# Squares averaged in two fp32r products and clamps of two operations, in a block of time mixing and a gated layer

## The reference

```python
xn = layernorm(x)
# time mixing (rwkv): shifted = rows one step later, zero in the first
k = (xn * mk + shifted * (1 - mk)) @ Wk       # v and r alike, with mv and mr
r = sigmoid(r_in @ Wr)
# per channel, over 512 steps, with td = -exp(decay), tf:
#   running maximum mx, numerator num and denominator den
#   out = (exp(mx - m) * num + exp(k + tf - m) * v) / (exp(mx - m) * den + exp(k + tf - m))
s = (r * out) @ Wo
# gated layer, expert 0 alone
h = relu(xn @ w1 + b1); y = xn + h @ w2 + b2
n = (y - mean(y)) * rsqrt(var(y) + eps) * gamma + beta
result = x + s * silu(n)
```

## Time and profile before

| what | us |
|---|---|
| median of 3 runs (lowest to highest) | 123.34 (123.24 to 123.43) |
| profiled execution, its own time | 122.89 |
| its span, first to last instruction | 121.0 |
| TensorE busy | 105.6 |
| VectorE busy | 96.4 |
| ScalarE busy | 95.0 |
| GpSimd busy | 79.8 |

### The profile page before, as it was taken

The page is one execution under the profiler, slowest core; times in us unless marked ns, Lnnn a source line. Parts: engine busy times, 40 slices in busy tenths (PEclk is TensorE's granted clock), DMA queues, the critical chain, the costliest instruction groups (busy, mean ns, idle before and its releaser), DMA issues. The chain is left out here.

```text
span 121.0 us, 1604 instructions
## 1 busy us (share of the span) xinstructions
PE 105.6 (87%) x336; PEld 56.7 (47%) x336; DVE 96.4 (80%) x199; ACT 95.0 (79%) x155; POOL 79.8 (66%) x104
## 2 busy tenths in 40 slices
...
GB/s 112 270 312 250 12 3 0 5 0 0 0 3 3 0 0 0 0 0 0 0 0 0 87 93 1 0 0 0 0 3 0 3 0 86 1 87 87 5 105 155
DMA packets 9449, 5.09 MB, mean 42 GB/s; under 512 B 480, under 2 KB 9184, under 8 KB 9440
## 3 DMA queue, kind: packets, MB, share of 16 engines
...
q10 hardware_dynamic: 560, 0.40, 1.3%
...
## 5 line engine op out<-in xcount | busy, mean ns | idle before, releaser
L632 PE MATMUL bank<-hid,w_c 128*128 128x512 f32 x64 | 31.4, 594 | 0.0
L581 PE MATMUL bank<-mixed,w_in 128*128 128x512 f32 x48 | 25.4, 624 | 1.7 <-DVE prod L792 0.6
L468 ACT ACTIVATE hid<-bank,vec 128x512 f32<-128x512 f32 x32 | 21.4, 681 | 2.3 <-PE bank L603 1.9
L601 PE MATMUL bank<-xT_hi,w_hi 128*128 128x512 f32 x28 | 16.5, 588 | 5.3 <-POOL xT_lo L356 5.3
L712 DVE SCALAR_TENSOR_TENSOR mixed<-step_x,vec,bank 128x511 f32<-128x511 f32 x24 | 17.5, 736 | 1.1 <-POOL step_x L365 1.1
L632 PEld LDWEIGHTS bank<-hid,w_c 128*128 128x128 f32 x64 | 12.2, 194 | 10.9 <-issue 9.7
L736 DVE TENSOR_TENSOR_SCAN den<-e_keep,bank 128x512 f32<-128x512 f32 x8 | 9.7, 1216 | 8.2 <-ACT e_keep L512 3.9
L389 POOL TENSOR_SCALAR gap_max<-gap,td 128x512 f32<-128x512 f32 x8 | 12.5, 1561 | 3.8 <-DVE gap L729 3.8
L581 PEld LDWEIGHTS bank<-mixed,w_in 128*128 128x128 f32 x48 | 8.4, 194 | 11.9 <-issue 8.8
L382 POOL TENSOR_SCALAR gap_min<-gap,td 128x512 f32<-128x512 f32 x8 | 12.5, 1561 | 1.9 <-DVE gap L729 1.9
L365 POOL TENSOR_TENSOR step_x<-xT 128x512 f32<-128x512 f32 x8 | 9.0, 1127 | 6.4 <-ACT xT L460 6.3
...
...
## 6 DMA issues: line engine op xcount, KB each, us to landing
...
```

Of the source, the lines that this page charges most:

```text
L468: act.activation(hid[b % 2][:, f, :], ps(f"up{f}", b)[:, :], ACT.Relu, bias=vec[:, B1_COLUMN + f:B1_COLUMN + f + 1]).then_inc(done[f"hid{f ...
L581: pe.matmul(ps(name, b)[:, :], w_in[:, which, :], mixed[b % 2][:, which, :], start=True, stop=True).then_inc(done[name], 1)
L601: pe.matmul(dst, hi, xT_hi[n][:, :], start=True, stop=False)
L632: ins = pe.matmul(ps("z", b)[:, :], w2_c[:, f, :], hid[b % 2][:, f, :], start=False, stop=last, skip_group_check=True)
```

## The change

Four things change together. First, for batches 0 to 6 the squares are split by GpSimd as the activations are: `sq_hi` is the square rounded to fp32r, `sq_lo` the rest, also stored as fp32r, and `var` becomes two fp32r products with `averager_r`, an fp32r copy of the averager, which add up in one bank. The halves of batch 7 keep the single fp32 product. Second, the two clamps are written with two operations each: a minimum and then a maximum, where the one that isn't needed compares with the largest fp32 number. Third, each `z` chunk has a semaphore of its own; `hid` of a chunk waits for that chunk's product of two batches ago, and `sq` for the last chunk in TensorE's list. Fourth, the lists of all four engines and the bank table are new.

The lists, in full but for that of ScalarE, whose start is shown:

```diff
     "pe": """
-        T:0 up3:0 b2m up2:0 k:0 T:1 up0:0 up1:0 v:0 k:1 up1:1 up0:1 up2:1 z0:0 z1:0 T:2 up3:1 z2:0 z0:1
-        z1:1 z3:0 up3:2 r:0 z3:1 z2:1 k:2 var:0 up2:2 up0:2 v:1 up1:2 z2:2 T:3 z0:2 var:1 s:0 z1:2 r:1
-        v:2 z3:2 up3:3 up2:3 up0:3 r:2 T:4 k:3 up1:3 z0:3 z2:3 var:2 z1:3 k:4 z3:3 up3:4 up0:4 var:3
-        up1:4 s:1 T:5 back:0 up2:4 v:3 back:1 z1:4 v:4 z0:4 up3:5 up1:5 z3:4 z2:4 T:6 s:2 r:3 r:4 k:5
-        up2:5 var:4 up1:6 up2:6 up0:5 v:5 T:7 k:6 z0:5 s:3 z2:5 up0:6 z1:5 z3:5 r:5 up3:6 z2:6 k:7 var:5
-        z1:6 up3:7 z0:6 up1:7 z3:6 up0:7 back:2 var:6 v:6 s:4 up2:7 back:3 v:7 z0:7 back:4 z1:7 z2:7 r:6
-        r:7 z3:7 s:5 var.a:7 var.b:7 back:5 s:6 s.a:7 back:6 s.b:7 back.a:7 back.b:7
+        T:0 up3:0 b2m up1:0 k:0 up0:0 T:1 v:0 up2:0 k:1 up2:1 up0:1 up1:1 up3:1 z3:0 T:2 r:0 z2:0 z1:0
+        z0:0 z3:1 z2:1 up0:2 z0:1 z1:1 up2:2 v:1 k:2 var:0 up1:2 z0:2 up3:2 T:3 z1:2 var:1 z2:2 v:2 r:1
+        z3:2 up0:3 up3:3 up1:3 up2:3 T:4 k:3 z3:3 r:2 z1:3 k:4 s:0 var:2 z2:3 z0:3 up3:4 up0:4 s:1 up2:4
+        T:5 v:3 z3:4 var:3 back:0 z2:4 back:1 z0:4 up1:4 v:4 up2:5 up0:5 z1:4 r:3 T:6 up3:5 r:4 up1:5
+        k:5 v:5 s:2 var:4 z1:5 up3:6 up2:6 z0:5 back:2 T:7 z2:5 s:3 up0:6 z3:5 up1:6 k:6 up0:7 r:5 z3:6
+        k:7 var:5 up2:7 z2:6 z0:6 z1:6 up3:7 up1:7 s:4 v:6 var:6 back:3 z3:7 s:5 back:4 v:7 z2:7 z1:7
+        z0:7 r:6 r:7 var.a:7 var.b:7 back:5 s:6 back:6 s.a:7 s.b:7 back.a:7 back.b:7
     """,
     "act": """
-        ln_exp ve:0 rs:0 xT:0 neg_td w1_hi ve:1 rs:1 hid3:0 xT:1 hid0:0 hid2:0 wo hid1:0 v_sb:0 ve:2
-        rs:2 e_keep:0 hid1:1 hid0:1 e_new:0 hid2:1 e_new:1 e_keep:1 xT:2 ln_den:0 hid3:1 ln_den:1
-        silu_set th_g:0 th_a:0 hid3:2 th_a:1 sq:0 th_g:1 th_r:0 ln_exp ln_var:0 hid2:2 rstd2:0 hid0:2
...
+        ln_exp ve:0 rs:0 wo neg_td xT:0 w1_hi ve:1 rs:1 xT:1 hid3:0 ve:2 rs:2 v_sb:0 hid1:0 hid2:0
+        hid0:0 e_new:0 hid2:1 hid0:1 e_keep:0 hid3:1 e_new:1 e_keep:1 xT:2 hid1:1 ln_den:0 ln_den:1
+        silu_set th_g:0 th_a:0 sq:0 th_a:1 hid0:2 th_r:0 th_g:1 sq:1 hid2:2 v_sb:1 ln_exp ln_var:0
...
     "dve": """
-        bnA:0 bnB:0 aggr1:0 norm1:0 bn:1 aggr1:1 ink:0 w2_sum cols bn:2 bn:3 aggr1:2 mx:0 inv:0 aggr1:3
-        ink:1 gap:0 inr:0 mx:1 bn:4 gap:1 inv:1 den:0 inr:1 den:1 aggr1:4 rel:0 ink:2 rel:1 inv:2 bn:5
-        dev:0 adev:0 wkv:0 aggr1:5 gated:0 mx:2 inr:2 gap:2 bn:6 zn:0 bn:7 aggr1:6 aggr1:7 dev:1 den:2
-        adev:1 wkv:1 rel:2 zn:1 inv:3 prod:0 ink:3 gated:1 inr:3 dev:2 adev:2 mx:3 wkv:2 gap:3 ink:4
-        gated:2 inv:4 mx:4 den:3 zn:2 gap:4 inr:4 rel:3 prod:1 res:0 den:4 zn:3 ink:5 res:1 rel:4 inv:5
-        dev:3 adev:3 wkv:3 dev:4 adev:4 wkv:4 gated:3 prod:2 gated:4 mx:5 gap:5 inr:5 ink:6 inv:6 zn:4
-        den:5 mx:6 rel:5 inr:6 prod:3 ink:7 dev:5 adev:5 gap:6 wkv:5 gated:5 mx:7 gap:7 den:6 inr:7 zn:5
-        inv:7 res:2 den:7 prod:4 rel:6 zn:6 res:3 rel:7 dev:6 adev:6 res:4 wkv:6 dev:7 gated:6 prod:5
-        adev:7 wkv:7 res:5 gated:7 prod:6 zn.a:7 zn.b:7 res:6 prod.a:7 prod.b:7 res.a:7 res.b:7
+        bnA:0 bnB:0 aggr1:0 norm1:0 bn:1 aggr1:1 ink:0 bn:2 w2_sum bn:3 aggr1:2 cols aggr1:3 inv:0 mx:0
+        ink:1 gap:0 bn:4 mx:1 inr:0 gap:1 inv:1 den:0 bn:5 den:1 inr:1 rel:0 rel:1 bn:6 aggr1:4 bn:7
+        dev:0 adev:0 ink:2 wkv:0 aggr1:5 gated:0 inv:2 inr:2 mx:2 gap:2 zn:0 aggr1:6 aggr1:7 dev:1 den:2
+        adev:1 zn:1 wkv:1 rel:2 inv:3 gated:1 ink:3 inr:3 dev:2 mx:3 ink:4 adev:2 gap:3 wkv:2 mx:4 gap:4
+        prod:0 gated:2 inr:4 zn:2 den:3 inv:4 prod:1 den:4 rel:3 inv:5 res:0 zn:3 ink:5 res:1 rel:4
+        dev:3 adev:3 wkv:3 dev:4 adev:4 gated:3 wkv:4 inr:5 mx:5 gap:5 gated:4 inr:6 prod:2 inv:6 den:5
+        zn:4 res:2 rel:5 prod:3 ink:6 ink:7 dev:5 mx:6 adev:5 gap:6 wkv:5 mx:7 gap:7 gated:5 inv:7 zn:5
+        den:6 inr:7 den:7 rel:6 prod:4 res:3 zn:6 res:4 rel:7 dev:6 prod:5 adev:6 wkv:6 dev:7 adev:7
+        gated:6 wkv:7 res:5 gated:7 prod:6 zn.a:7 zn.b:7 res:6 prod.a:7 prod.b:7 res.a:7 res.b:7
     """,
     "pool": """
-        d:0 w1_lo nm:1 fix:0 norm1:1 w2_c d:1 xT_hi:1 fix:1 xT_lo:1 gmax:0 nm:2 gmin:0 norm1:2 gmin:1
-        gmax:1 dv:0 d:2 xT_hi:2 xT_lo:2 keep:0 fix:2 norm1:3 keep:1 gmax:2 gmin:2 dv:1 d:3 xT_hi:3 nm:4
-        fix:3 xT_lo:3 norm1:4 dv:2 keep:2 xT_hi:4 d:4 fix:4 gmin:3 gmax:3 xT_lo:4 norm1:5 norm1:6 gmax:4
-        gmin:4 norm1:7 xT_hi:5 d:5 xT_lo:5 dv:3 keep:3 dv:4 keep:4 xT_hi:6 fix:5 xT_lo:6 d:6 fix:6
-        gmin:5 gmax:5 xT_hi:7 dv:5 d:7 keep:5 fix:7 gmax:6 xT_lo:7 gmin:6 gmin:7 gmax:7 dv:6 keep:6 dv:7
-        keep:7
+        d:0 w1_lo nm:1 fix:0 norm1:1 w2_c nm:2 d:1 xT_hi:1 fix:1 xT_lo:1 gmin:0 gmax:0 norm1:2 gmin:1
+        gmax:1 dv:0 d:2 fix:2 xT_hi:2 xT_lo:2 keep:0 sq_hi:0 norm1:3 sq_lo:0 sq_hi:1 sq_lo:1 keep:1 dv:1
+        gmax:2 gmin:2 nm:4 xT_hi:3 d:3 xT_lo:3 norm1:4 fix:3 dv:2 keep:2 d:4 sq_hi:2 fix:4 sq_lo:2
+        xT_hi:4 gmin:3 xT_lo:4 gmax:3 gmax:4 norm1:5 gmin:4 sq_hi:3 sq_lo:3 xT_hi:5 d:5 xT_lo:5 dv:3
+        norm1:6 keep:3 dv:4 keep:4 fix:5 sq_hi:4 sq_lo:4 xT_hi:6 d:6 xT_lo:6 gmin:5 gmax:5 norm1:7 dv:5
+        fix:6 xT_hi:7 d:7 xT_lo:7 keep:5 sq_hi:5 fix:7 sq_lo:5 gmax:6 gmin:6 gmin:7 gmax:7 sq_hi:6
+        sq_lo:6 dv:6 keep:6 dv:7 keep:7
     """,
...
```

The bank table is rewritten; in it `b2m` is followed by `v:0` in its bank, where `z:1` followed before, and a check of the bank is added ahead of `b2m`. The rest of the diff:

```diff
@@ -138,6 +141,7 @@
 
         ident = sb("ident", P, P)
         averager = sb("averager", P, P)
+        averager_r = sb("averager_r", P, P, dt=FP32R)
         vec = sb("vec", P, NV)
         neg_td = sb("neg_td", P, 1)
         td = sb("td", P, 1)
@@ -187,6 +191,8 @@
         gated = pair("gated", P, T)
         hid = pair("hid", P, NF, T)
         sq = pair("sq", P, T)
+        sq_hi = pair("sq_hi", P, T, dt=FP32R)
+        sq_lo = pair("sq_lo", P, T, dt=FP32R)
         ln_var = pair("ln_var", P, T)
         rstd2 = pair("rstd2", P, T)
         zn = pair("zn", P, T)
@@ -211,7 +217,7 @@
                   "mx", "gap", "gmin", "gmax", "e_new", "e_keep", "den", "ln_den", "rel",
                   "th_g", "th_a", "keep", "dv", "dev", "adev", "wkv", "th_r", "gated", "s"]
                  + [f"up{f}" for f in range(NF)] + [f"hid{f}" for f in range(NF)]
-                 + ["z", "sq", "var", "ln_var", "rstd2", "zn", "silu", "prod", "back", "res"])
+                 + [f"z{f}" for f in range(NF)] + ["sq", "sq_hi", "sq_lo", "var", "ln_var", "rstd2", "zn", "silu", "prod", "back", "res"])
         done = {n: sem(f"done_{n}") for n in STEPS}
         stored = [sem(f"stored_{n}") for n in range(2)]
         EDGES = 11
@@ -242,6 +248,10 @@
             elif previous:
                 for step in FREED_BY[previous[0]]:
                     after(eng, step, previous[2], previous[1])
+
+        def chunks_of(b):
+
+            return [name for name, _, i in tokens("pe") if name in CHUNKS and i == b]
 
         def cut(half):
             return {"": slice(0, T), "a": slice(0, T // 2), "b": slice(T // 2, T)}[half]
@@ -309,6 +319,8 @@
                                base=0, pattern=[[-1, P]], channel_multiplier=1).then_inc(prep["ident"], 1)
             pool.memset(eps[:, :], LN_EPS).then_inc(prep["consts"], 1)
             pool.memset(averager[:, :], 1.0 / H).then_inc(prep["consts"], 1)
+            pool.wait_ge(prep["consts"], 2)
+            pool.tensor_copy(averager_r[:, :], averager[:, :]).then_inc(prep["consts"], 1)
 
             def center_w2():
                 pool.wait_ge(prep["w2_sum"], 1)
@@ -379,14 +391,16 @@
                 once(pool, b, "cols", 4)
                 after(pool, "gap", b)
                 after(pool, "e_new", b - 2)
-                pool.tensor_scalar(gap_min[n][:, :], gap[n][:, :], td[:, :], None, ALU.min).then_inc(done["gmin"], 1)
+                pool.tensor_scalar(gap_min[n][:, :], gap[n][:, :], td[:, :], -FP32_MAX,
+                                   ALU.min, ALU.max).then_inc(done["gmin"], 1)
 
             def upper(b):
                 n = b % 2
                 once(pool, b, "cols", 4)
                 after(pool, "gap", b)
                 after(pool, "e_keep", b - 2)
-                pool.tensor_scalar(gap_max[n][:, :], gap[n][:, :], td[:, :], None, ALU.max).then_inc(done["gmax"], 1)
+                pool.tensor_scalar(gap_max[n][:, :], gap[n][:, :], FP32_MAX, td[:, :],
+                                   ALU.min, ALU.max).then_inc(done["gmax"], 1)
 
             def value_steps(b):
                 n = b % 2
@@ -403,7 +417,20 @@
                 after(pool, "dev", b - 2)
                 pool.tensor_scalar(keep[n][:, 1:], th_g[n][:, :], -0.5, 0.5, ALU.mult, ALU.add).then_inc(done["keep"], 1)
 
-            steps = {"w1_lo": w1_low, "w2_c": center_w2, "nm": minus_mean_rows, "norm1": normalise, "xT_hi": high_part,
+            def square_high(b):
+                n = b % 2
+                after(pool, "sq", b)
+                after(pool, "var", b - 2)
+                pool.tensor_copy(sq_hi[n][:, :], sq[n][:, :]).then_inc(done["sq_hi"], 1)
+
+            def square_low(b):
+                n = b % 2
+                after(pool, "sq_hi", b)
+                after(pool, "var", b - 2)
```

(38 more changed lines are left out.)

32 lines of the change are left out of this document (18 added, 14 removed).

## The result

The changed kernel takes 112.56 us (112.39 to 112.66, four runs) against 123.37 of before: a ratio of 0.912, 95% interval 0.911 to 0.914, so 10.8 us less. I had forecast 117.3 and a range of 114.5 to 121.8. The direction was right, and the gain is nearly twice what I took. The profiled execution took 112.47, with a span of 110.6. Where some executions of a kernel ran in a slower state of the chip, the times and ratios here leave them out.

What follows compares the result with a forecast made beforehand. It took GpSimd's queue in two places, TensorE's slower clock behind them, and TensorE with ScalarE from 60 on to bound the kernel. Of 11.2 us, ScalarE's cap left 6.0: 123.3 - 6.0 = 117.3, range 114.5 to 121.8.

Steps and rivals of the forecast that it cites:

- The price of the clamp: On GpSimd, a two-operation clamp takes 0.66 us instead of 1.56, judged by the nearest rows in form; 16 save 14.4.
- The first and second wait: TensorE's waits for `xT_lo` of batches 2 and 4, behind GpSimd's clamps: 2.57 goes and 1.89 all but goes.
- The slow clock: TensorE's lower granted clock after its two long waits: 1.68 and 1.70 us lost, to go with the waits.
- The averages: Squares' average on TensorE, batches 0 to 6: two fp32r products replace one fp32, 0.39 less each, 2.7 us in all.
- The sum: Of 11.2 us to be had on TensorE, 6.0 kept, since ScalarE's and VectorE's work doesn't shrink and ScalarE caps the gain.
- my own formula: Middle, 20 to 105 us: ScalarE's 73.5 busy divided by its busy share; at 93% it lasts 79.0, a gain of 6.0.
- My inventory of 11.2: TensorE's possible savings: 2.7 averages, 2.57, 1.89 and 0.67 waits for `xT_lo`, 1.68 and 1.70 slow clock.
- The signs: Expected profile: clamps 0.6 to 0.8, average records 0.24 apart, `xT_lo` waits under 1.5, clock above 0.98, ScalarE above 90%.
- the cap of 93%: ScalarE, 86% busy from 20 to 105 us, was allowed 93% over the whole middle, limiting the gain to 6.0.
- The slow clamp with the split squares: Rival on GpSimd: clamps keep 1.56 while squares add 13.1 to 13.7 us; near 128, chance 0.13.
- Squares that come late: Rival: clamps fast, but squares delayed in GpSimd's queue cost 4 plus 1.7 slow clock; 121.5 to 123, chance 0.12.
- Collisions: Rival: `sq_lo` and the cast on GpSimd meet VectorE's scan, 4.7 us more GpSimd work; 119, chance 0.15, gain kept.

Runs made afterwards that it cites:

- The forms: Changed kernel with another clamp form in each of batches 2 to 6, for durations alone; one execution, 125.58 us, a time that means nothing.
- filling the waits: Kernel before with 9 and 7 useless small products in TensorE's two long waits for `xT_lo`; 122.22 us, ratio 0.993.

## Why the prediction was wrong

*The price of the clamp* was right (0.69 for 0.66), its reason wrong. I wrote that the form of two operations was the nearest row. The forms show that the pair decides; by my reason a maximum then a minimum would be as fast, and it takes 2.0. The Trainium skill's best loop ("GPSIMD Engine Reference", §3.1), 0.77 for 512 elements, was above both 0.62 and 0.69 as measured.

*The first and second wait* went as worked out, the first to about half a microsecond in place.

*The slow clock* at 1.68 + 1.70 was a mis-sized term: 0.9 as measured by filling the waits.

*The averages* shortened as predicted on TensorE (0.46 for the two records in place of 0.86), but the 2.7 were not to be had: with unsplit squares the new lists take 112.2, no more than with split ones.

*The sum* has the step that failed: "ScalarE is thus the engine that caps the gain, and I take 6.0". I took ScalarE's busy share of 86% as its own property and allowed it 93%. Much of its idle time was made by the clamps, 8.5 us of it in the list of waits, of which I had used for ScalarE only the 1.5 for `var`; the change took 7.2 of the 8.5 away. Its share rose to 96.6%. At that share my own formula gives 73.5 / 0.966 = 76.1, a gain of 8.9 in the middle. The other 1.5 us of the span came outside it, where the sum had nothing: 0.8 is less busy time of ScalarE, the rest less idle time. My inventory of 11.2 was near the measured 10.8 by luck: 8.5 for waits and clock was at most 7.2, 2.7 for the averages was about nothing, and 4.2 from the other clamps, most likely through ScalarE, was missing.

*The signs* that I named for the changed kernel came out as written but for the 0.24 between the two records: clamps at 0.69, no wait for `xT_lo`, a clock of 1.000, ScalarE above 90%. They test the clamps and the two waits, and none of them tests the cap of 93%.

*The rivals.* The slow clamp with the split squares: 128 forecast; with the new lists it is 123.2, no slower than before, and in the old lists 133.2. Squares that come late: true of the old lists (122.5), where the price was 10.7 and not 4; the new lists avoid it. Collisions exist: in the changed kernel a `sq_hi` at 27.30 took 1.27 where 0.61 is usual, beside VectorE's scan of two tiles, and another at 66.44 took 1.42, beside the same scan; `sq_lo` was never longer than 1.29. On the squares that is 1.5 us in all and not 4.7. What it costs in time no run shows.
